# One kernel, four layers: expert choice planned inside the attention's last pair, x and weights in quarters, stores straight to their rows

## What is computed

```
x = x + attention(layernorm(x))          # 16 heads of 64, causal, 2048 tokens
x = x + experts(layernorm(x))            # 8 experts 128->512->128, gelu, one expert per token
x = x + linear_attention(layernorm(x))   # 16 heads of 8, running sums
x = x + experts(layernorm(x))            # same expert weights
```

## Time and profile before

| | us |
|---|---|
| runs: median of 3 (lowest, highest) | 1268.22 (1266.94, 1268.91) |
| profiled execution: its own time | 1268.68 |
| its span | 1267.0 |
| first score matmul begins | 34.2 |
| last statistics of the attention end | 975.3 |
| first slot of expert layer 1 is loaded | 1014.8 |
| last store of expert layer 1 is issued | 1066.0 |
| linear attention begins | 1076.4 |
| expert layer 2 begins | 1165 |
| its last store is issued | 1257.1 |

### The profile page before, as it was taken

One profiled execution on the slowest core, in us unless ns is written; L12 is line 12 of the kernel. 1 busy time (PEld: TensorE's weight loads), 2 busy tenths in 40 slices (PEclk: granted clock), 3 DMA queues, 4 the chain that ended last, 5 costly groups with the idle time before them and its releaser, 6 DMA issues. The chain is left out here.

```text
span 1267.0 us, 24526 instructions
## 1 busy us (share of the span) xinstructions
PE 1143.7 (90%) x8010; PEld 854.2 (67%) x8010; DVE 939.8 (74%) x2101; ACT 796.7 (63%) x2192; POOL 841.2 (66%) x809
## 2 busy tenths in 40 slices
PE   5899999999999999999999999999996486786386
PEld 4577677677767776776777677767774386454386
DVE  5877877878787778777878877787784464698465
ACT  5777777767777777767777677777762153442243
POOL 1587677857786766678577958666685544684545
PEclk9999999999999999999999999999999588798588
DMA  4100620080026006300800170020014132000132
GB/s 121 46 2 1 187 65 2 18 242 2 1 66 187 1 1 157 104 2 1 239 13 1 51 210 1 1 67 2 1 57 106 67 98 81 1 1 1 67 96 84
DMA packets 71404, 77.66 MB, mean 61 GB/s; under 512 B 8272, under 2 KB 59600, under 8 KB 71216
## 3 DMA queue, kind: packets, MB, share of 16 engines
q1 hardware_dynamic: 68272, 68.84, 20.2%
q0 software_dynamic: 3008, 7.25, 1.6%
HBM read 16.39 MB, written 43.96 MB: 48 GB/s over the span
## 5 line engine op out<-in xcount | busy, mean ns | idle before, releaser
L387 DVE TENSOR_REDUCE at_nmax<-at_ps 128x1 f32<-128x512 f32 (+3 forms) x640 | 373.6, 602 | 126.2 <-PE at_ps L555 123.3
L359 POOL TENSOR_SCALAR at_prob<-at_prob,at_scale 128x512 f32<-128x512 f32 (+3 forms) x312 | 429.2, 1393 | 1.8
L469 ACT ACTIVATE at_prob<-at_ps,at_nmax 128x512 f32<-128x512 f32 (+3 forms) x416 | 259.4, 630 | 45.5 <-DVE at_nmax L387 43.4
L552 PE MATMUL at_ps<-at_k_st,at_q_parts 128*128 128x512 f32 (+3 forms) x640 | 283.5, 443 | 4.9 <-DVE at_k_st L443 2.6
L581 PE MATMUL at_ps<-at_probT,at_v 128*64 128x256 f32 (+1 forms) x2304 | 270.3, 374 | 1.4 <-DVE at_probT L410 1.3
L482 ACT ACTIVATE at_probT<-at_ps 128x512 f32<-128x512 f32 (+1 forms) x288 | 165.2, 573 | 140.5 <-PE at_ps L566 129.1
L555 PE MATMUL at_ps<-at_k_st,at_q_parts 128*128 128x512 f32 (+3 forms) x640 | 252.9, 395 | 0.0
L359 POOL TENSOR_SCALAR late<-late,at_scale 128x512 f32<-128x512 f32 (+1 forms) x168 | 226.2, 1362 | 1.6
L410 DVE COPY at_probT<-at_ps 128x512 f32<-128x512 f32 (+1 forms) x288 | 188.8, 655 | 50.9 <-PE at_ps L566 48.3
L566 PE MATMUL at_ps<-ident,at_prob 128*128 128x128 f32 x1440 | 219.7, 274 | 3.0 <-DVE at_probT L410 1.8
L581 PEld LDWEIGHTS at_ps<-at_probT,at_v 128*64 128x64 f32 x2304 | 152.5, 136 | 102.3 <-issue 41.0
(11 more groups left out here) (193 smaller groups left out, 1502.4 us busy)
## 6 DMA issues: line engine op xcount, KB each, us to landing
slots_in<-zeros SPq DMA_DIRECT2D x6, 2967.0 KB, 18.4
slots_in<-zeros SPq DMA_DIRECT2D x6, 2838.0 KB, 17.8
at_q_parts<-at_q_parts SPq DMA_DIRECT2D x64, 256.0 KB, 3.7
f_xs<-slots_in SPq DMA_DIRECT2D x46, 129.0 KB
late<-in_L_ffn_w_dram SPq DMA_DIRECT2D x1, 2048.0 KB, 9.1
late<-in_L_ffn_w_dram SPq DMA_DIRECT2D x4, 512.0 KB, 6.4
rows<-slots_out SPq DMA_DIRECT2D x4, 256.0 KB, 3.6
out_dram<-slots_out SPq DMA_DIRECT2D x4, 256.0 KB, 3.5
```

What stands on the lines that cost most here:

```text
L359: pool.tensor_scalar(cols, cols, scale[:, k, u, c:c + 1], None, ALU.mult).then_inc(s_fix["pool"], 1)
L387: dve.tensor_reduce(nmax[:, q % 2, 2 * i + h, c:c + 1], bank, AX.X, ALU.max, negate=True).then_inc(s_max, 1)
L469: act.activation(prob[ROW_HOME[j]][u][:, c * BANK:c * BANK + w], ring[use_of["score", p, j, i, h, c] % RING][:, 0:w], ACT.Exp, bias=nmax[: ...
L552: pe.matmul(bank[:, 0:w], q_hi[h][:, r * P:(r + 1) * P], keys, start=True, stop=False)
```

## The change

The diff has some 1,080 lines; these are its parts.

1. **Planner.** A table `WEIGHT` scales ten kinds of step durations; a change between value and other PE steps is charged 0.3 one way instead of 0.16 both ways. So the order of every engine's steps changes in all 8 pairs.
2. **Prologue.** The set-up block is gone; its steps stand at the head of the attention's DVE and POOL queues. x comes in four DMAs, the first tiles of the Q, K and V weights on their own. Statistics, root, norm (two tiles of four on POOL) and the 13 groups of transposes (`set`) are planned steps; a projection waits only for its own groups. Pair 0 takes its rows and chunks in ascending order.
3. **Choice of expert layer 1.** It is planned in the attention's last pair, for batches of tiles in the order in which rows finish; the roots of batches 0 to 2 are taken after six rows, that of batch 3 after the last. The scatters are planned POOL steps of lowest priority. Slot starts and experts are found at the end of DVE's attention queue.
4. **Stores.** Tokens carry their own row as target. Rows without a token carry 2048, and the indirect DMA skips targets over 2047. Expert layer 2 writes the output itself; layer 1 writes `new_x`, which is loaded into x in four DMAs that nobody waits for in that layer: the linear attention's statistics wait for each quarter.
5. **Loop.** The eviction of the transposed slot (L853) goes from DVE to ACT.

```
+WEIGHT = {("pe", "score"): 1.1, ("pe", "value"): 0.93, ("pe", "turn"): 0.88, ("pe", "project"): 0.87, ("pe", "out"): 1.04,
+          ("act", "evict"): 0.91, ("dve", "low"): 0.92, ("dve", "add"): 1.16, ("pool", "fix"): 1.04, ("act", "leave"): 1.07}
...
+ROOTS = {0: 3, 3: 4}
+def rows_in_order(p):
+    return ROW_ORDER if p else tuple(sorted(ROW_ORDER))
...
+    for b in range(NC):
+        if b in ROOTS:
+            step(("groot", b), "act", 2.9 if b < NC - 1 else 1.6, ("dve", "gate0"), ("dve", "add") + everything[2 * ROOTS[b] - 1 - STEPS])
...
+        step(("gnorm", b), "dve", 1.4, ("act", "groot", max(a for a in ROOTS if a <= b)))
+        step(("gturn", b), "pe", 0.5, ("dve", "gnorm", b), ("pe", "gate2"))
+        step(("gturn", b), "act", 0.6, ("pe", "gturn", b), ("pe", "gate2"))
+        step(("glogit", b), "pe", 0.5, ("act", "gturn", b), ("dve", "gate3"))
+        step(("gchoose", b), "dve", 1.2, ("pe", "glogit", b))
+        step(("gexp", b), "act", 0.25, ("dve", "gchoose", b))
+        step(("grank", b), "pe", 0.6 + 0.25 * b, ("dve", "gchoose", b))
+        step(("gplace", b), "dve", 1.3, ("pe", "grank", b), ("act", "gexp", b))
+        for i in range(TPC):
+            step(("gscatter", b, i), "pool", 1.27, ("dve", "gplace", b))
...
-              "pool": ["gap", "weigh", "scale", "fix"], "sp": ["second"]}
+              "pool": ["norm", "gap", "weigh", "scale", "fix", "gscatter"], "sp": ["second"]}
...
-                length += 0.16 * ((s[1] == "value") != (last == "value"))
+                length += 0.3 * (s[1] != "value" and last == "value")
...
+                sp.dma_start(x[:, 0:TPC, :], x_rows[:, 0:TPC, :]).then_inc(s_xin[0], 16)
+                for n in "qkv":
+                    sp.dma_start(wnat[n][:, 0:1, :], weights[n][:, 0:1, :]).then_inc(s_win["p"], 16)
...
-                rows = scratch_out[SLOTS * P:SLOTS * P + T, :]
...
-                sp.wait_ge(s_out, 16 * NC)
+                if reload:
+                    rows = out.rearrange("(c t p) d -> c p t d", p=P, t=TPC)
+                    for c in range(NC):
+                        sp.dma_start(x[:, TPC * c:TPC * (c + 1), :], rows[c]).then_inc(keep["s_x"][c], 16)
...
-                    pool.indirect_dma_start(scratch_out[:, :], bass.IndirectOffsetOnAxis(ap=back[k][:, :], axis=0),
-                                            ys[k][:, :], None).then_inc(s_store[k], 16)
+                    pool.indirect_dma_start(out, bass.IndirectOffsetOnAxis(ap=back[k][:, :], axis=0),
+                                            ys[k][:, :], None, bounds_check=T - 1, oob_is_err=False).then_inc(s_store[k], 16)
...
-                in_turn({"xT": 1, "weights": 0, "y": 3, "mix": 2}, emit)
+                in_turn({"weights": 0, "y": 3, "mix": 2}, emit)
...
-                in_turn({"gelu": 2}, emit)
+                in_turn({"xT": 1, "gelu": 2}, emit)
```

More of the change, by code:

```diff
@@ L55, with chunks_in_order, set_of @@
 CHUNK_ORDER = (0, 2, 1, 3)
+WEIGHT = {("pe", "score"): 1.1,
+          ("pe", "value"): 0.93,
+          ("pe", "turn"): 0.88,
+          ("pe", "project"): 0.87,
+          ("pe", "out"): 1.04,
+          ("act", "evict"): 0.91,
+          ("dve", "low"): 0.92,
+          ("dve", "add"): 1.16,
+          ("pool", "fix"): 1.04,
+          ("act", "leave"): 1.07}
+SETS = ("p0", "x0", "x1", "x2", "x3", "o0", "q1", "k1", "v1", "q2", "k2", "v2", "o1")
+ROOTS = {0: 3, 3: 4}
+def rows_in_order(p):
+    return ROW_ORDER if p else tuple(sorted(ROW_ORDER))
+def chunks_in_order(p):
+    return CHUNK_ORDER if p else tuple(sorted(CHUNK_ORDER))
+def set_of(what, p):
+    if what == "x":
+        return SETS.index(f"x{p}")
+    if what == "o":
+        return SETS.index(f"o{p // 4}")
+    return SETS.index(what + str((p + 3) // 4) if p else "p0")
 def attention_plan(PAIRS, NT, NC, TPC):
     STEPS = NT // 2
-    everything = [(p, j) for p in range(PAIRS) for j in ROW_ORDER]
+    everything = [(p, j) for p in range(PAIRS) for j in rows_in_order(p)]
     place = {pj: q for q, pj in enumerate(everything)}
@@ L118, in attention_plan @@
             w = width(j, i, c) / BANK
-            step(("score", p, j, i, h, c), "pe", max(0.43 * w, 0.2) + 0.2 * (c == n - 1),
+            step(("score", p, j, i, h, c), "pe", max(0.46 * w, 0.21) + 0.14 * (c == n - 1),
                  ("dve", "low", p, c, 0), ("sp", "second", p, 2 * j // TPC))
             step(("max", p, j, i, h, c), "dve", 0.15 + 0.54 * w, ("pe", "score", p, j, i, h, c), q > 1 and ("pool", "scale") + everything[q - 2])
-            step(("exp", p, j, i, h, c), "act", 0.42 + 0.46 * w, ("dve", "max", p, j, i, h, c), old and ("pe", "turn") + old + (1, old[1]))
+            step(("exp", p, j, i, h, c), "act", 0.42 + 0.46 * w, ("dve", "max", p, j, i, h, c), old and ("pe", "turn") + old + (1, old[1]),
+                 ("act", "root", NC - 1), not old and ROW_HOME[j] < 2 and ("act", "set", len(SETS) - 1))
         last = ("act", "exp", p, j) + score_steps(j)[-1]
@@ L149, in attention_plan @@
         step(("leave", p, j), "act", 0.4, ("pe", "value", p, j, j))
-        step(("out", p, j), "pe", 0.44, ("act", "leave", p, j))
+        step(("out", p, j), "pe", 0.44, ("act", "leave", p, j), has_set("o", p))
         step(("add", p, j), "dve", 0.45, ("pe", "out", p, j))
-    reader = {"score": ("act", "exp"), "project": ("dve", "low"), "vproject": ("act", "vproject"), "out": ("dve", "add")}
-    urgent = {"pe": ["out", "project", "vproject", "score", "turn", "value"],
-              "act": ["factor", "leave", "evict", "vproject", "high", "exp"],
-              "dve": ["peak", "total", "fix", "evict", "low", "max", "add"],
-              "pool": ["gap", "weigh", "scale", "fix"], "sp": ["second"]}
+    last_score = "pe", "score", PAIRS - 1, everything[-STEPS][1], 0, 0, 0
@@ new lines, in attention_plan @@
+    reader = {"score": ("act", "exp"), "project": ("dve", "low"), "vproject": ("act", "vproject"), "out": ("dve", "add"), "set": ("act", "set"),
+              "gate1": ("dve", "gate2"), "gate2": ("dve", "gate3"), "gturn": ("act", "gturn"), "glogit": ("dve", "gchoose"), "grank": ("dve", "gplace")}
+    urgent = {"pe": ["out", "grank", "glogit", "gturn", "gate1", "gate2", "project", "vproject", "score", "set", "turn", "value"],
+              "act": ["root", "set", "factor", "leave", "evict", "gturn", "vproject", "high", "groot", "gexp", "exp"],
+              "dve": ["norm", "stat", "peak", "total", "fix", "evict", "low", "max", "add", "gplace", "gchoose", "gnorm", "gate0", "gate1", "gate2", "gate3"],
+              "pool": ["norm", "gap", "weigh", "scale", "fix", "gscatter"], "sp": ["second"]}
@@ L213, in attention @@
     order, everything, place, group, row_before, chunks, width, score_steps, turned, fixer, run_of = attention_plan(PAIRS, NT, NC, TPC)
-    uses = [it for it in order["pe"] if it[0] in ("score", "project", "vproject", "out")]
+    uses = [it for it in order["pe"] if it[0] in ("set", "score", "project", "vproject", "out", "gate1", "gate2", "gturn", "glogit", "grank")]
     use_of = {it: n for n, it in enumerate(uses)}
@@ L447, in _ @@
                         last.then_inc(s_lo, 1)
+                find_slots(dve, link, shp, keep, count[:, :].unsqueeze(2), over, small, passed, moved,
+                           keep["slot_row"][:, :], keep["slot_e"][:, :], keep["s_slot"])
             @block.scalar
             def _(act):
-                act.wait_ge(s_aggr, NT)
-                act.activation(rstd[:, :], mv[:, :, 1], ACT.Sqrt, bias=keep["eps"][:, 0:1]).then_inc(s_std, 1)
-                W_GROUPS = PAIRS // TPC
-                dst = [w[:, TPC * i:TPC * (i + 1), :] for w in (wT["q"], wT["k"], wT["v"], wo) for i in range(W_GROUPS)]
@@ L455, in _ @@
[L455 to L459 removed]
+                act.wait_ge(keep["s_z"], 1)
+                act.activation(zT[0][:, 0:1], keep["eps"][:, 0:1], ACT.Sqrt)
@@ L944, in rank @@
                     last.then_inc(s_rank, 1)
[L946 to L962 removed]
+                if not scattered:
+                    turn(0)
                     for c in range(1, NC):
```

576 lines of the change are left out of this document (369 added, 207 removed).

## The result

The changed kernel takes 1251.0 us (median of 4 runs, 1249.67 to 1252.47) against 1267.93 (1266.94 to 1268.91) for the kernel before on the same chip: ratio 0.9867, 95% interval 0.985 to 0.9884. The gain is 17 us where 33.5 were forecast, and the time lies 3 us above the range. The profiled execution spans 1249.1 us against 1267.0, and the 17.9 us between them split as follows. The stages are bounded by instructions that stand in both traces: row 1's last add, the end of the last statistics (those of the last row of the attention), the first expert matmul, the last store's issue, the first statistics of the linear attention, the last store of layer 2, the span's end.

What follows compares the result with a forecast made beforehand. PE was taken to bound 60 to 952 us, leaving gains only where PE waits. Terms -9 + 1 + 2 - 16.9 - 4.2 - 6.4 = -33.5 took 1268.68 to 1235.2, median 1234.7 us; range 1225 to 1248.

Steps and rivals of the forecast that it cites:

- Prologue, -9: Kernel start up to 60 us: earlier x loads cut PE's lost time from 20.3 to 11 us; ends 4 and 15.
- Boundary, "0 to 3; I take 1": Change from pair 0 to 1: only row 7's turns cover pair 1's projections, costing 1 us.
- Middle, 0: Attention pairs up to 952 us: new planner weights reorder every pair at no net cost; bounds -4 and +6.
- Tail, +2, bounds 0 to 6: Attention's end: about 6 us of choice work against 2.2 us of PE idle costs 2 us.
- planned steps disturb the tail and the middle: Rival: evicts wait behind chooses (+4 more), prologue gives only 5 (+4), total 1243 us; chance 0.20.
- Choice, -16.9: Choice of expert layer 1: last statistics to first expert matmul falls from 43.1 to 26.2 us.
- no unexplained wait: Rival: the rank result is read without the unrecorded wait, 4.7 us less, total 1230 us; chance 0.15.
- the barrier (1.0, E+19.5): Attention block's end: barrier takes 1.0 us, over 19.5 us after E, the end of the last statistics.
- Loop, 0: Expert slot loop: PE holds the pace at 1.89 us a slot, ACT's added eviction and the stores' skip test cost nothing.
- POOL against DVE: Rival: tail scatters take 1.37 us beside DVE; with the rank's wait gone too, total 1232 us; chance 0.05.
- Linear start, -4.2: Start of linear attention: statistics begin at 1072.2 once the first quarter lands, 4.2 us gained; bounds 3 and 4.8.
- End, -6.4: Program end: no output copy, a closing barrier of 1.1 us, end at 1260.6 instead of 1267.0; bounds 5.9 and 6.7.

Runs made afterwards that it cites:

- Edit 3: Changed kernel with pair 0's rows ordered 1, 2, 3, 4, 5, 6, 7, 0; 1250.2 us, ratio 0.986 to the kernel before.
- edit 5: Changed kernel with the expert choice's PE steps behind value and turn in the planner's priorities; 1248.47 us, ratio 0.9829 to the kernel before.
- Edit 4: Changed kernel with all planned expert-choice steps behind the attention's steps in every engine's queue; 1264.84 us, ratio 0.9978 to the kernel before.
- edit 7: Changed kernel with POOL holding its scatters in the attention's last pair until batch 2 is placed; ratio 0.9892 to the kernel before.
- edit 8: Changed kernel with batch 2's rank (PE) and placing (DVE) moved behind row 0's output and add; 1248.99 us, ratio 0.9839 to the kernel before.
- edit 6: Changed kernel with POOL starting expert layer 2's scatters only when all four batches are placed; 1261.61 us, ratio 0.9954 to the kernel before.
- number 13: Changed kernel with edits 3, 5 and 9 together; 1240.11 us, ratio 0.9813 to the kernel before.
- number 14: Changed kernel with edits 3, 8 and 9 together; 1243.83 us, ratio 0.9833 to the kernel before.
- edit 1: Changed kernel with pair 0's rows back to 4, 3, 5, 2, 6, 1, 7, 0; 1250.51 us, ratio 0.985 to the kernel before.
- edit 2: Changed kernel with pair 0's rows ordered 2, 3, 4, 5, 6, 1, 7, 0; 1252.33 us, ratio 0.9854 to the kernel before.
- edit 9: Changed kernel with batch 3's four scatters and the slot finding moved to the first expert layer's block; 1252.34 us, ratio 0.9884 to the kernel before.

## Why the prediction was wrong

The sign, the bound of the middle and most terms held. Two steps failed, the tail and the boundary of pair 0. The tail missed by 13.9 us and the start up to row 1's add by 5.9, which together make 19.8; 4.2 came back elsewhere, and 15.6 is what the forecast missed by.

- **Prologue, -9.** First score matmul at 24.2 (forecast 20), idle up to 60 us 13.2 (forecast 11). With the clock the gain is 7.1, inside 4 to 15. ACT's terms, 9.6 + 10 + 2.6, make 22 and not the "about 21" of the sum.
- **Boundary, "0 to 3; I take 1".** The failed step. It was seen that row 7 alone covers pair 1's projections, but that was priced by an amount of work. 3.6 us went as idle of PE, and 3.5 more were lost by a half clock behind two waits of 1.0 and 1.7 us: 7.1. Edit 3 brought 4.1 back at row 4's add of the last pair and 2.4 at row 1's. By edit 5, where the clock stayed full, its half was worth some 1.5 in the end. So the start to row 1's add gave 2.15 instead of 8, and even that arose in the last pair.
- **Middle, 0.** 3.1 us idle in 800; the pairs 2 to 6 are alike. It holds up to the last pair, where the new order gave 3.0.
- **Tail, +2, bounds 0 to 6.** The step that failed most: it took 15.9. The sum counted PE's 6 us of choice work against its idle time and the queues as if steps could pass each other. The rival "planned steps disturb the tail and the middle" named the mechanism and priced it at +4. Edit 4 shows that all but 0.4 of it comes with the planned steps. Edits 7 and 8 took away 4.6 and 4.4 us, of which the hold of PE at batch 2's rank makes 2.9 by the rows of edit 7 and the full clock 1.7. The rest is turns and evictions behind logits, exp and table load, and the half clock from 970 on; how it splits between these two wasn't measured.
- **Choice, -16.9.** It gave 18.75. From E to the last scatter's end 13.6 us passed, not 18.5: no scatter ran beside batch 3's rank, so the 4.8 us of unexplained wait that were carried over weren't there. That was the rival "no unexplained wait", right in its term and wrong in its total. Against this, "the barrier (1.0, E+19.5)" was 4.0. These are two errors of 4.9 and 3.0 with opposite signs. From the block's start to the first expert matmul it took 6.8, and 6.7 were forecast.
- **The table load.** It takes 1.28 us; the ACTIVATE before it ends at 969.31, 0.01 ahead, and the exp begins 0.01 after it (969.32 + 1.28, then 970.61). The Trainium skill (ScalarE: Activation LUTs, "What ACT_TABLE_LOAD costs") adds a drain of 1.38 us to a switch; here too the rows have no room for it.
- **Loop, 0.** +0.65, of which the clock makes 0.5: it rose 4.2 us after the first expert matmul, against 3.3 before. Of the 46 stores 42 take 0.98 to 0.99 us and four, all in layer 1, 1.32 to 1.60; the longest of them with 0.30 behind it just fills the 1.9 of a slot. The 1.37 of the rival "POOL against DVE" is gone in the median, though the copy of 1156 columns is still DVE's (L1099). It now begins together with the store (1039.34 and 1039.35) and no longer 0.5 us into it (1040.39 and 1039.90 in the kernel before).
- **Linear start, -4.2.** It gave 5.0. The start didn't wait for the first quarter, as forecast, but for POOL's exit (4.36); the sum came near by chance.
- **End, -6.4.** It gave 4.8: the failed step is "a closing barrier of 1.1"; the end lies 4.1 behind the last store.
- **Layer 2, 0.** It gave 3.7 that no step foresaw. The linear attention's span from first to last matmul is 85.0 before and 83.6 after; among fourteen kernels with the same code in it eight have 83.1 to 83.8 and six 84.9 to 85.1. So 1.5 of it is not the change's. The second loop took 49.6 before, with the clock at full 9 us after its first matmul, and 48.1 after, with 3 us; the same code has 48.1 to 48.2 in nine of the fourteen and 49.9 to 50.4 in five. So neither is this 1.4 the change's, and 0.8 are left.

## What to carry to other kernels

In queues that run in order a step costs more than its length: it costs what everything behind it waits while it waits, so place extra steps by what stands behind them and look at the wait they bring along, not at the idle time they fill. When an operation is removed from the path, ask what it had hidden; here a copy and its wait had hidden 4 us of POOL's exit at the end of each expert layer. A loss seen at one place (7 us at the boundary) is worth at the end only what the next stages let through (4.1 at one row, 2.4 at the last), and only an experiment shows it. Where a planner lays out the whole program, an edit of one part changes the order in all the others, so look for what else moved before its result is put down to the edit. And trace the same queues more than once: nine traces of one order differ here by 3 us.

## What was not expected of the hardware

- **A rank can be held while POOL's indirect DMAs run.** With none in flight DVE never waited more than 0.75 us for its result; with some it waited 1.1 to 7.7 in most traces (1.12 and 5.76 in layer 2 of the changed kernel, 7.71 in edit 4), and edits 6 and 7 moved the wait with the scatters. But some ranks with scatters beside them have 0.4 to 0.75, above all in numbers 13 and 14, where the same code is not held. So the scatters are needed for it in all that was seen and are not enough. Which resource they share is open. PE's records show none of it.
- **The hold of PE went with its clock.** The fp32 matmuls behind batch 2's rank were held too. With the same steps around it the idle before row 0's output is 3.50, 3.53 and 3.50 us where PE was at half clock throughout (the changed kernel, edits 1 and 3) and 6.45, 6.42 and 6.89 where it was back at full by 980 (edits 2, 6 and 9); the tails are 39.1 and 40.6 to 40.9 us. Which of the two brings the other, or whether a third thing brings both, is open.
- **POOL's next step comes 3.6 to 4.4 us after its last indirect DMA where a block ends behind it** (3.55 in edit 3 to 4.36 at the end of layer 1). It is 1.2 for the whole barrier where the last one lies 8.5 us back.
- **The clock's rise differs.** With the same loop PE's granted clock went from 1.2 to 2.4 GHz between 3 and 9 us after the first expert matmul, in stretches of 1 us. Where it came within 5 us the first loop took 48.1 to 48.3 us, where it came after 8 us 50.0 to 50.3 (layer 2's: 48.1 to 48.2 and 49.9 to 50.4). Nothing in these traces says which it will be. Edits of 2 us must be read from a place ahead of it, here h, or from many runs.
